# Routing of the first mixture of experts, pair by pair inside the attention before it

## The reference

```python
x = x + tanh(g_xattn[0]) * xattn_0(layernorm(x), ctx, ctx, mask0)
x = x + tanh(g_ffn[0])   * ffn_0(layernorm(x))     # top 2 of 8 experts, capacity
x = x + tanh(g_xattn[1]) * xattn_1(layernorm(x), ctx, ctx, mask1)
x = x + tanh(g_ffn[1])   * ffn_1(layernorm(x))     # top 2 of 8 experts, no capacity
# in ffn_0: T = 1600 tokens, CAP = 500
logits = xt @ w_g; top_v, top_i = top_k(logits, 2)
exp_rank = cumsum(one_hot(top_i) of all first choices, then of all second ones) - 1
# a choice counts only where its rank within its expert is below CAP
out = sum over a token's choices of probs * gelu(row @ c_fc[e]) @ c_proj[e]
```

## Time and profile before

| | us |
|---|---|
| median of 3 runs | 1683.66 (1682.76 to 1684.49) |
| the profiled execution | 1681.74 |
| its span in the trace | 1679.9 |

### The profile page before, as it was taken

One profiled execution on the slowest core, in us unless ns is written; L12 is line 12 of the kernel. 1 busy time (PEld: TensorE's weight loads), 2 busy tenths in 40 slices (PEclk: granted clock), 3 DMA queues, 4 the chain that ended last, 5 costly groups with the idle time before them and its releaser, 6 DMA issues. The chain is left out here.

```text
span 1679.9 us, 35318 instructions
## 1 busy us (share of the span) xinstructions
PE 1311.7 (78%) x10632; PEld 1041.5 (62%) x10633; DVE 869.0 (52%) x2918; ACT 810.1 (48%) x2219; POOL 308.4 (18%) x337
## 2 busy tenths in 40 slices
PE   3699999984089998059999999999999973049970
PEld 2576676664078888057787878787878753026650
DVE  3466666664035544446665656665665656302223
ACT  3588778773044543136554555555545544013320
POOL 2333333310700000711000000000000000430016
PEclk9899999995589999569999999999999995579995
DMA  5811000000232320220000000000000000822113
GB/s 138 346 29 27 26 26 26 27 2 0 78 139 100 134 104 26 74 83 11 21 11 11 10 10 10 10 10 10 10 10 0 1 1 0 319 60 66 62 58 107
DMA packets 42626, 92.25 MB, mean 55 GB/s; under 512 B 10205, under 2 KB 30877, under 8 KB 39261
## 3 DMA queue, kind: packets, MB, share of 16 engines
q1 hardware_dynamic: 32468, 77.37, 13.6%
q0 software_dynamic: 8192, 13.15, 2.8%
q10 hardware_dynamic: 1872, 0.68, 0.3%
HBM read 66.18 MB, written 24.97 MB: 54 GB/s over the span
## 5 line engine op out<-in xcount | busy, mean ns | idle before, releaser
L507 ACT ACTIVATE b_prob<-b_prob,b_low 100x361 f32<-100x361 f32 x256 | 155.6, 608 | 108.0 <-DVE b_low L596 108.0
L364 PE MATMUL b_ps_p<-b_context_part,b_wk_part 128*128 128x362 f32 x768 | 157.7, 342 | 0.0
L1046 ACT ACTIVATE a_prob<-a_prob,a_low 100x361 f32<-100x361 f32 x256 | 154.2, 605 | 4.4 <-DVE a_low L1164 4.4
L515 ACT COPY b_prob_t<-b_ps_t 128x300 f32<-128x300 f32 x256 | 103.8, 406 | 104.2 <-PE b_ps_t L420 101.3
L370 PE MATMUL b_ps_p<-b_wv_part,b_context_part 128*128 128x512 f32 (+1 forms) x576 | 151.6, 406 | 0.0
L596 DVE CUSTOM_DVE_ANT_0 b_prob<-b_ps_s,b_mask_bias 100x361 f32<-100x361 f32 x256 | 121.3, 532 | 45.3 <-PE b_ps_s L410 30.0
L1164 DVE CUSTOM_DVE_ANT_0 a_prob<-a_ps_s,a_mask_bias 100x361 f32<-100x361 f32 x256 | 121.5, 532 | 34.8 <-PE a_ps_s L947 34.8
L420 PE MATMUL b_ps_t<-ident,b_prob 100*128 100x100 f32 x768 | 117.1, 261 | 22.1 <-ACT b_prob_t L515 21.5
L1054 ACT COPY a_prob_t<-a_ps_t 128x300 f32<-128x300 f32 x256 | 97.7, 409 | 67.7 <-PE a_ps_t L957 64.8
L364 PEld LDWEIGHTS b_ps_p<-b_context_part,b_wk_part 128*128 128x128 f32 x768 | 124.6, 189 | 0.3 <-issue 0.2
L420 PEld LDWEIGHTS b_ps_t<-ident,b_prob 100*128 100x128 f32 x768 | 78.1, 141 | 66.3 <-issue 52.4
(11 more groups left out here) (205 smaller groups left out, 2530.5 us busy)
## 6 DMA issues: line engine op xcount, KB each, us to landing
rows_in<-zero SPq DMA_DIRECT2D x16, 512.0 KB, 13.9
w<-in_c_fc SPq DMA_DIRECT2D x8, 1024.0 KB, 6.3
w<-in_c_proj SPq DMA_DIRECT2D x8, 1024.0 KB, 4.9
f_w<-in_W SPq DMA_DIRECT2D x2, 4096.0 KB
a_context<-in_ctx SPq DMA_DIRECT2D x16, 361.0 KB, 3.6
b_context<-in_ctx SPq DMA_DIRECT2D x16, 361.0 KB
f_xe<-rows_in SPq DMA_DIRECT2D x8, 512.0 KB, 3.9
rows_out<-f_ye SPq DMA_DIRECT2D x8, 512.0 KB, 3.0
```

Source lines behind the costliest of these rows:

```text
L364: ins = nc.tensor.matmul(bank[:, 0:LN2], w_parts["k"][a][:, k, t * P:(t + 1) * P], cx_parts[s][b][:, k, :], start=m == 0, stop=m == DK * l ...
L507: nc.scalar.activation(prob[0:S, k, 0:L], prob[0:S, k, 0:L], ACT.Exp, bias=low[0:S, k:k + 1], scale=-1.0, accum_out=total[0:S, k:k + 1]).t ...
L515: nc.scalar.copy(pt[:, k % PAIR_PT, :], ps_t[:, 0:KT_N * S]).then_inc(pt_ready.sem, 1)
L1046: nc.scalar.activation(prob[0:S, k, 0:L], prob[0:S, k, 0:L], ACT.Exp, bias=low[0:S, k:k + 1], scale=-1.0, accum_out=total[0:S, r:r + 1]).t ...
```

## The change

The first mixture's routing moves into `attention_first`; `normalise` n1 goes, and `feed_forward(0)` is replaced by `experts_first`, whose loop over the experts computes the same. A new class `Router` has the operations of one pair (two batches). `first_schedule` gets three new unit kinds, all of the pair before (N in slot 5, G in slot 6, C in slot 7), an empty unit in slot 4, and W of batch 1 moves from slot 4 to slot 3. The last pair does its N, G and C in three slots of their own at the end.

Since second choices can't be ranked until all first choices are counted, each expert now has two lists in DRAM, one per choice, and SyncE appends the second list to the first, with a DRAM-to-DRAM copy of 512 rows per expert, before it loads the rows. The DRAM buffer of layer 0 is larger, so `load_later` zeroes it with 16 transfers of 512 KB and the buffer of layer 1 with 8. GpSimd's walk over the pairs is unrolled, and it begins after the wait for the zeroing of layer 0's buffer. Cut to its core:

```diff
+class Router:
+    LINKS, STRIDE = (3, 7), 2 * SLOTS
+    def moments(self, dve, averaged):          # DVE, slot 4, after the four find_max
+        self.apart(dve)
+        for s in range(2):
+            ins = self.nc.vector.bn_aggr(self.mv[0:S, s, :], self.st[0:S, s, :])
+        ins.then_inc(averaged.sem, 1)
+    def power(self, tile, exponent):
+        e = self.T["exponents"][0:S, EXPONENTS.index(exponent), :]
+        return self.nc.gpsimd.tensor_tensor(tile[0:S, :], tile[0:S, :], e, ALU.pow)
+    def scales(self, pool, j):                 # POOL, slot 4
+        if j:
+            pool.wait_ge(self.dispatched, 64 * j)
+        pool.wait_ge(self.averaged.sem, self.averaged.at(j, 1))
+        self.pool_own.link(pool, g.tensor_scalar(self.rs[r, :], self.mv[r, :, 1], LN_EPS, None, ALU.add))
+        self.pool_own.link(pool, self.power(self.rs, -0.5))
+        self.make_shift(pool, self.scaled)     # two more of 100x2
+    def make_rows(self, act, j):               # ACT, end of slot 4
+        act.wait_ge(self.scaled.sem, self.scaled.at(j, 1))
+        for s in range(2):
+            ins = self.nc.scalar.activation(self.rows[0:S, s * D:(s + 1) * D], x of batch 2j+s,
+                                            ACT.Identity, scale=self.rs[...], bias=self.shift[...])
+        ins.then_inc(self.rowed.sem, 1)
+    def turn(self, pe, bank, j):               # N: four transposes of 100x128
+    def keep_turned(self, dve, bank):          # 128x400 from PSUM
+    def score(self, pe, bank):                 # G: 2 batches x 2 matmuls, 8 columns
+    def keep_logits(self, dve, bank):          # 100x16 from PSUM
+    def choose(self, dve, j):                  # 2 max, 2 max_index, a copy, 2 is_equal of 100x16
+    def note(self, pool, j):                   # POOL: two copies of 100x16 and 100x4
+    def rank_rows(self, pe, bank, j):          # C: two matmuls, 32 columns each
+    def keep_counts(self, dve, bank):          # 128x64 from PSUM
+    def route(self, pool, j):                  # POOL: 16 operations, 13 of them waited for one by one
+        own.link(pool, g.tensor_tensor(run[:, :, 1, :], run[:, :, 0, :], tot[:, :, 0, :], ALU.add))
+        own.link(pool, g.tensor_tensor(rank[r, :, :, :], within[r, :, :, :], run[r, :, :, :], ALU.add))
+        ...
+        own.link(pool, g.tensor_copy(self.scat[r, :, :], self.row[r, :, :]))
+        pool.sem_inc(self.routed.sem, 1)
+    def scatter(self, pool, rows_in):          # POOL: four indirect DMAs of 100 rows
...
 def first_schedule(last):
-    at = [[] for _ in range(QUADS + QUAD_VALUE + 3)]
+    at = [[] for _ in range(QUADS + QUAD_VALUE + 5)]
-    at[3] += [("K", 1, 1, 0), ("V", 1, 2, 0)]
-    at[half].append(("W", 1, 0, -1))
+    at[3] += [("K", 1, 1, 0), ("V", 1, 2, 0), ("W", 1, 0, -1)]
+    at[ROUTE_AT + 1].append(("N", 0, 0, -1))
     at[half + QUAD_VALUE].append(("R", 0, 0, 0))
+    at[ROUTE_AT + 2].append(("G", 0, 0, -1))
...
-    at[7] += [("K", 0, 1, 0), ("Q", 0, 1, 0), ("V", 0, 2, 0)]
+    at[7] += [("K", 0, 1, 0), ("Q", 0, 1, 0), ("V", 0, 2, 0), ("C", 0, 0, -1)]
...
+    for k in range(-sum(len(slot) for slot in at) % FIRST_BANKS):
+        at[ROUTE_AT].append(("none", 0, k, 0))
...
             def steps(i, sched):               # GpSimd
-                for p in range(QUADS):
+                for p in range(len(sched.slots)):
                     if sched is full and p == half:
                         convert(0, i + 2, maxed.at(i, H))
                     for u, unit in sched.slots[p]:
                         if unit[0] in ("Q", "K"):
                             lower(unit, sched.split[u], i, False)
-                if sched is full:
-                    convert(1, i + 2, maxed.at(i, HEADS))
+                    j = routed_pair(i, p)
+                    if j is not None:
+                        router.scales(pool, j)
+                    if sched is full and p == QUADS - 1:
+                        convert(1, i + 2, maxed.at(i, HEADS))
+                    for u, unit in sched.slots[p]:
+                        if no_outputs(i, unit[3]):
+                            continue
+                        if unit[0] == "G":
+                            router.note(pool, i + unit[3])
+                        elif unit[0] == "C":
+                            pool.wait_ge(taken.sem, taken.at(i, u + 1))
+                            router.route(pool, i + unit[3])
+                            router.scatter(pool, D_["xs0"])
...
-            iterations(pool, steps)
+            pool.wait_ge(D_["cleared"][0], D_["cleared_value"][0])
+            for i in range(PAIRS):
+                steps(i, full if i < PAIRS - 1 else final)
...
         def append(e, s):                      # SyncE, experts_first
+            have = sp.value_load(T["firsts"][0:1, bass.ds(e, 1)], min_val=0, max_val=SLOTS)
+            sp.dma_start(XS[bass.ds(have + e * STRIDE, SLOTS), :]..., XS[bass.ds(e * STRIDE + E * STRIDE, SLOTS), :]...
+                         ).then_inc(merged[s], 16)
...
+            sp.wait_ge(T["summed"][0], 1)
+            sp.wait_ge(T["dispatched"][0], 16 * 2 * B)
+            for s in range(2):
+                append(s, s)
+            for s in range(2):
+                sp.wait_ge(merged[s], 16)
+                load_rows(s, s)
...
     def load_later(sp):
-        for n in (0, 1):
-            X = D_[f"xs{n}"][0:ROWS, :].rearrange("(g p j) d -> g p (j d)", p=P, j=4)
-            for g in range(ROWS // P // 4):
-                sp.dma_start(X[g, :, :], zero[:, :]).then_inc(D_["cleared"], 16)
+        for g in range(2 * E):
+            sp.dma_start(X[g, 0, :, :], zero[:, :]).then_inc(D_["cleared"][0], 16)
+        ...
+        for g in range(E):
+            sp.dma_start(X[g, :, :], zero[:, :]).then_inc(D_["cleared"][1], 16)
...
-    normalise(nc, T, "n1_", False, False, "wr0")
-    feed_forward(nc, 0, T, D_, out)
+    experts_first(nc, T, D_)
```

More of the change, by code:

```diff
@@ L730, in attention_first @@
     n_units, n_pre = len(full.units), len(pre.units)
+    router = Router(nc, T, 0, sb)
+    T["dispatched"].append(router.dispatched)
+    T["summed"].append(router.summed)
     scored = Counted(nc, nm + "scored", QUADS)
@@ L911, in project @@
                     return
+                elif kind == "N":
+                    ins = router.turn(pe, bank, i + p)
+                elif kind == "G":
+                    pe.wait_ge(taken.sem, taken.at(i, sched.units.index(("N", 0, 0, p)) + 1))
+                    ins = router.score(pe, bank)
+                elif kind == "C":
+                    ins = router.rank_rows(pe, bank, i + p)
                 elif kind == "R":
@@ new lines, in _, with keep_rows, gelu, keep_hidden @@
+        @block.scalar
+        def _(act):
+            for k in (xt_ready, gelu_done, ht_ready):
+                k.credit(act)
+            exps(act)
+            def keep_rows(i, s):
+                wait(act, x_turned, i, s + 1)
+                wait(act, up_done, i, s - 1)
+                nc.scalar.copy(xt[s][:, :, :].rearrange("p k s -> p (k s)"), ps[s][:, 0:DK * P]).then_inc(xt_ready.sem, 1)
+            def gelu(i, s):
+                wait(act, b1_added, i, s + 1)
+                wait(act, h_turned, i, s - 1)
+                nc.scalar.activation(hg[s][:, :], hb[s][:, :], ACT.Gelu_apprx_tanh).then_inc(gelu_done.sem, 1)
+            def keep_hidden(i, s):
+                wait(act, h_turned, i, s + 1)
+                wait(act, down_done, i, s - 1)
+                nc.scalar.copy(ht[s][:, :, :].rearrange("p f s -> p (f s)"), ps[4 + s][:, :]).then_inc(ht_ready.sem, 1)
+            last = TILES // 2 - 1
+            keep_rows(0, 0)
+            gelu(0, 0)
+            keep_rows(0, 1)
+            keep_hidden(0, 0)
+            gelu(0, 1)
+            keep_rows(1, 0)
+            with act.Fori(1, last) as i:
+                keep_hidden(i - 1, 1)
+                gelu(i, 0)
+                keep_rows(i, 1)
+                keep_hidden(i, 0)
+                gelu(i, 1)
+                keep_rows(i + 1, 0)
+            keep_hidden(last - 1, 1)
+            gelu(last, 0)
+            keep_rows(last, 1)
+            keep_hidden(last, 0)
+            gelu(last, 1)
+            keep_hidden(last, 1)
@@ new lines, in _, with add_b1, add_b2 @@
+        @block.vector
+        def _(dve):
+            for k in (b1_added, y_ready):
+                k.credit(dve)
+            route(dve)
+            dve.wait_ge(w_in, 64)
+            def add_b1(i, s):
+                expert = dve.value_load(owner_i[0:1, bass.ds(2 * i + s, 1)], min_val=0, max_val=E - 1)
+                wait(dve, up_done, i, s + 1)
+                wait(dve, gelu_done, i, s - 1)
+                nc.vector.tensor_tensor(hb[s][:, :], ps[2 + s][:, :], b1[:, bass.ds(expert * F1, F1)],
+                                        ALU.add).then_inc(b1_added.sem, 1)
+            def add_b2(i, s):
+                expert = dve.value_load(owner_i[0:1, bass.ds(2 * i + s, 1)], min_val=0, max_val=E - 1)
```

(13 more changed lines are left out.)

982 lines of the change are left out of this document (591 added, 391 removed).

## The result

The changed kernel took 1695.3 us (median of four runs, 1691.1 to 1697.8) against 1683.2 for the kernel before in the same session (four runs, 1680.5 to 1684.5): ratio 1.0065, 95% interval 1.0043 to 1.0088. It is **slower by 0.65%**, and 29 us above the forecast of 1666. The chip of this measurement is not on record. The profiled run took 1691.1 us with a span of 1689.3.

A forecast was written before the change was run, and what follows sets the result against it. TensorE was taken to bound attention and expert loop, with an unoverlapped 87.1 us chain between. Gap -55, start +10 and pairs +27 sum to -18 from 1681.7, 1663.7; the median stands 1.9 higher: 1666 us, range 1646 to 1688.

The forecast's parts named there:

- four scatters at 0.99 + 0.30: 5.2: In a pair, behind GpSimd's ranks: four scatters issued in a row occupy GpSimd for 5.2 us.
- I add nothing for company: Scatters beside VectorE's work: 1018 ns against 990 alone in the trace, so no extra time was added.
- Start: Zeroing ahead of the second pair's context grows from 16 to 24 transfers: 10.0 us more, bounds 8 and 12.
- Pairs: New routing work in the attention's pairs: 3.0 us in seven and 1.0 in six, 27 us more, bounds 13 and 50.
- Gap: From the last `bn_stats` to the first expert's rows: 32.1 us against 87.1, 55 us less, bounds 48 and 60.
- Slot 4 without a unit would be 2.75, less than VectorE's four maxima allow (about 3.1), so 0.4 is lost: Moving W out of slot 4 costs TensorE 0.4 us a pair, since VectorE's maxima limit the emptied slot.
- GpSimd's lateness: After ranks and scatters, GpSimd's lower key part delays VectorE's slot 3 key unit 1.5 us; 1.0 us in six pairs.
- Expert loop: An append of 512 KB per expert is hidden, since TensorE is the bound; nothing is taken there.
- Rival 2: The pair costs only its matmuls, 1.8 us in seven pairs, GpSimd and ScalarE being free in time: 1650 us; chance 0.20.
- Rival 3: GpSimd late for slot 3's key unit: each microsecond beyond 12.1 costs one in six pairs, so slower; chance 0.14.
- Rival 4: Shared port: scatters among VectorE's operations take say 2 us more each in six pairs, +48, 1714 us; chance 0.04.
- Rival 5: Work only moves: N waits for ScalarE and that for GpSimd, 2 us in seven pairs, 1680 to 1686 us; chance 0.07.

The follow-up runs named there:

- second measurement: The changed kernel as it is, run again on another chip, against the kernel before: 1670.3 us, ratio 0.9938.
- the first kernel of the first group: The changed kernel without the four scatters of pairs 0 to 6, the last pair's kept: 1665.4 us, ratio 0.9896.
- the best version: Changed kernel with batch 1's tile-2 value unit in slot 4, layer 1's zeroing behind the last context, GpSimd's scales before its mask conversion: 1651.5 us, repeated 1650.1.

## Why the prediction was wrong

The forecast of 1666.0 us missed the first measurement by 29 us, and the range (1646 to 1688) missed it too. In three repeats on three chips the changed kernel took 1669.4 to 1671.7 us, inside the range and 3 to 6 us above the forecast; in a fourth it took 1692.6.

**The step that failed** is "four scatters at 0.99 + 0.30: 5.2" in the pair, as time of GpSimd alone, hidden up to the key unit, with nothing for other engines. "I add nothing for company" asked only what company does to the scatter, and there it was right: 0.99 us each beside VectorE's maxima. It did not ask what the scatter does to its company. In the two measurements with the hold TensorE's results came 2.5 to 4 us late in each of pairs 3 to 7, and less in pair 2. Runs on one chip give the price: 1692.6 - 1668.7 = 24 us, and 1695.3 - 1670.3 = 25 across chips. The 32 scatters of the kernel before couldn't show it, since TensorE had nothing to do beside them. But its trace does show late results beside GpSimd's other indirect transfers, the gathers with which the first mixture ends (L1529, one every 1.3 us until 714.25). VectorE adds two terms to x there, L1539 and L1540, and the second waits for the first one's signal, mostly for nothing. Three times it waits long, and ScalarE waits for VectorE's `f_shift`, which is done at 709.82, from the timelines of the two:

```profile
711.74 2.08 ACT L1272 ACTIVATE xn<-x,f_shift,f_rs 100x256 f32<-100x256 f32 x4 [2.67 <-remote]
712.48 0.48 DVE L1540 SCALAR_TENSOR_TENSOR x<-f_got,f_weight,x 100x256 f32<-100x256 f32 x1 [2.27 <-issue]
715.27 0.48 DVE L1540 SCALAR_TENSOR_TENSOR x<-f_got,f_weight,x 100x256 f32<-100x256 f32 x1 [1.91 <-issue]
717.37 0.48 DVE L1540 SCALAR_TENSOR_TENSOR x<-f_got,f_weight,x 100x256 f32<-100x256 f32 x1 [1.22 <-DVE x L1539]
```

The first measurement of the changed kernel has the same three waits in its gathers (1.58, 1.94 and 1.21 us, behind 718 us), and no other profiled run has one above 0.6. So the sign was there to be read before, and it isn't TensorE's results alone that can come late.

Term by term, with the profile of the second measurement (no hold; span 1666.7 against 1679.9, so -13.2 where I had -18):

- *Start*, +10.0: right. The score moved from 81.98 to 92.18, and putting off the eight transfers gave 8.9 to 9.8 us in three pairs of kernels, each on one chip. "512 KB over the rate read in a full queue" was a sound price.
- *Pairs*, +27: the last `bn_stats` ends 38.0 us later, of which 27.8 are not the start. The sum was right by luck, since its parts were not. N, G and C with their hand-overs are 1.5 a pair, not 2.3. "Slot 4 without a unit would be 2.75, less than VectorE's four maxima allow (about 3.1), so 0.4 is lost" was the second failed step: the slot without a unit is 4.61 us, because TensorE then waits for a maximum and for a copy in turn, and the move costs 1.6. GpSimd's lateness costs nothing, not 1.0: its ranks took 5.3 us up to the first scatter instead of 6.9, as the small operations follow one another every 0.3 us and not every 0.44, and `a_keys_lo` is ready 0.9 us before its key unit. Falls of TensorE's clock behind the emptied slot, 5.0 us in this run, weren't in the sum at all.
- *Gap*, -55: it is 37.2 instead of 87.1 us, so -49.9. What I missed stands in front of the chain: the scatters of pair 6, and their landing, are still in GpSimd's queue when the last moments are ready. The timelines of VectorE, GpSimd and TensorE, second measurement, with both ends of the gap:

```profile
415.21 0.43 DVE L1406 BATCH_NORM_STATS2 a_st<-x 100x6 f32<-100x256 f32 x1
...
416.91 0.99 POOL L321 DMA_INDIRECT rows_in<-a_rows,a_scat  x1 [0.30 <-issue]
419.69 0.23 POOL L205 TENSOR_SCALAR a_rs<-a_mv 100x2 f32<-100x2 f32 x1 [1.79 <-DMA rows_in<-a_rows,a_scat]
...
452.84 1.97 PE L1860 MATMUL f_ps<-ident,f_xe 128*128 128x128 f32 x8 [24.17 <-DMA f_xe<-rows_in]
```

  The moments were ready at 416.0, so 3.6 us. Without that pair's scatters (the first kernel of the first group) the gap is 32.4 us, and I had 32.1, but again with two errors that cancel: the ranks are 1.6 us shorter than taken, and from the end of the last scatter to the issue of the append pass 4.6 us (439.34 to 443.93), where I had 1.7 for the landing and 0.3 for reading the count. The append takes 4.1 us from its issue to the first load of rows (443.93 to 448.03), forecast 4.5.
- *Expert loop*, 0: right, 177.3 us in both. From the first `up` to the end the two spans are within 1.4 us (1210.5 and 1209.2). That is less than what single runs differ by there: from the first turn of rows to the end the profiled runs take 1210.8 to 1220.9 us.

**The rivals.** Rival 2 (pairs under 42.5 us) is out, at 43.2. Rival 3 was priced well in the total (the run with 5.5 us more work on GpSimd came out 24.9 us slower than the changed kernel beside it, where (5.5 - 0.9) x 6 gives 27.6). It didn't decide, since GpSimd needs 10.3 us from the end of its conversion to the end of the scatters and not 12.1. Its sign and size matched the first measurement by chance. Rival 4 has the wrong victim. No scatter here was longer than 1.3 us. The Trainium skill ("SBUF — State Buffer", "Who interferes with whom") has GpSimd's descriptors wait for VectorE; no run here shows it. The same section says that a DMA never contends with a compute engine. In two of the measurements TensorE's results were late while indirect transfers were made (24 us in all), and with plain transfers on the same chip they were not. Whether that is contention in the section's sense isn't shown; that the engines lost time beside these transfers is measured, and the measurement decides. Rival 5: N waits 0.3 us for ScalarE, as taken.

**What stays open.** What in the chip makes the results late. The hold was seen in the first measurement (whose chip isn't known) and in one of the six groups after it; on the other five chips it was in none of the 14 profiled kernels with scatters among the pairs. Since each chip was measured in one group only, I can't tell whether it belongs to a chip or to something else that was going on at the time. The records can't say whether the array stands still or only its signals are late, since the ends of matmuls are modelled; that VectorE's own signals to itself were late beside the gathers speaks for the signals, and isn't proof. Nor is it shown that the gathers' delays and the hold are the same thing. Whether spread scatters or the best version escape the hold wasn't seen, as neither was measured where there was one.

## What to carry to other kernels

Before a part taken out is believed, run the changed kernel itself once more beside it, on the same chip: here three removals each "proved" the cause of a loss that the changed kernel, run again, didn't have. A unit moved out of a slot gives back only what the slot's next limit allows. Read that limit from the waits of the other engines in that slot, and count what an emptied slot does to TensorE's clock. When work is moved beside a busy engine, price both directions, what company does to the work and what the work does to its company, and look at what the moved work leaves in the queue in front of the next critical chain.

## What was not expected of the hardware

Four indirect transfers issued in a row by GpSimd (5.0 us) can go with a delay of up to 4 us in what TensorE hands to VectorE and ScalarE, in two of five measurements of the same kernel, for 24 us in a run of 1670. Plain transfers of the same amount to consecutive rows did not, on the same chip. Beside indirect gathers VectorE's wait for its own last result was up to 2.3 us long, in the kernel before and in one run of the changed one. And with every engine's work unchanged, two waits of 0.9 us on TensorE in one slot were followed, in some pairs, by a granted clock of 0.59 on average in the next slot, which made it 2.3 us longer; with one matmul unit moved into the waiting slot this was in none of four profiled runs.
